# Attention beside a two-of-eight expert layer: tokens routed in parts of 12 and 20 tiles, the top two by maxima, another order of the set-up, the experts' tiles without a loop

## The chip, the cores and the metric

The kernel runs on one core of a Trainium2 chip, as one launch. The metric is the device time of an execution in microseconds (us). TensorE (PE, with its weight loads as PEld), VectorE (DVE), ScalarE (ACT), GpSimd (POOL) and SyncE (SP) each run a program of their own and meet at semaphores; a name with a q (PEldq, ACTq, SPq) is what an engine's sequencer does itself, such as loading a register or issuing a DMA.

## The reference

`x` is (4, 1024, 128), that is 4096 tokens or 32 tiles of 128. `xn` is its layer norm.

```
out  = x + attention(xn) + experts(xn)
attention: xn / max(|xn|, 1e-12) * sqrt(128) * gamma @ w_qkv, 16 heads of 64,
           causal softmax(q k^T / 8) v, @ w_out
experts:   logits = xn @ Wr^T + br                       # 8 experts
           top_v, top_i = top_k(logits, 2); w = softmax(top_v)
           o = sum over the two chosen e of w_e * (relu(xn @ W1[e]^T + b1[e]) @ W2[e]^T + b2[e])
           result = layer_norm(xn + o) * ffn_gamma + ffn_beta
```

Of two equal logits the expert with the lower number counts as the greater.

## The kernel before, in words

There are three stretches. In the **set-up** `x` is normed, the weights are turned by TensorE (a "unit" is four 128x128 transposes into one of four PSUM banks), the router chooses two experts a token, and GpSimd scatters each token's row twice into `sorted_x` in HBM, sorted by expert and padded to whole tiles of 128 rows. In the **expert stage** 78 tiles are run through the two layers of the expert that owns them. In the **attention** the 16 heads of 4 sequences follow, and the experts' rows are gathered back meanwhile. A barrier stands between the expert stage and the attention.

The routing is done in two parts of 16 tiles, `REGION = 2 * 16 + 7 = 39` sorted tiles each. For a part VectorE takes the statistics (L471, L474), norms (`layernorm`, L479 to L493), TensorE makes the logits, four tiles (a group) at a time, from a turned and copied `xn` (L658, L396, L667), `router` (L517 to L534) ranks the eight logits of a token against each other in 1024-wide operations (L521 to L526), TensorE counts the chosen (L673, L674), `places` (L540 to L563) makes every row's place of it, and GpSimd issues 32 indirect DMAs (L350). `experts_and_weights` (L570 to L579) gives `tile_expert`, the expert of each sorted tile, and the mixing weights.

What order the set-up has is the list `units`, which TensorE (`turn`), ScalarE (`evacuate`, plus `normed` and `exponentials`) and VectorE (`lower`) all walk: router and bias weights, `xn` of the first half, `w1` of all experts, `w2` of all, `n` (the normed rows for the attention) of the first half, then `xn` and `n` of the second. A bank of kind `w1` or `n` is read twice, by ScalarE (rounded) and then by VectorE (the rest, `w1T_lo` L504, `nT_lo` L508), and is free after that. TensorE waits for the last four banks before the expert stage.

In the expert stage every engine runs `step(j, k, i)` for tile j. On TensorE (L699 to L746) a step reads the expert's number from SBUF into a register (`expert_of`, L278), turns the rows of tile j+1 (L709), turns the hidden layer of tile j-1 (L727), multiplies tile j by W1 in three passes (L734 to L736) and tile j-2 by W2 (L743). `expert_steps` writes steps 0 to 2 out, runs steps 3 to 74 in a hardware loop of 12 rounds with 6 steps, and writes steps 75 to 80 out. In the last four steps of a round the register that was loaded two steps earlier serves W2 too; in the first two it is loaded anew. SyncE loads the sorted rows, three tiles a time, into two slots (L304).

```
inside = i is not None and k >= FIRST + 2
e_out = tile_experts[k - 2] if inside else expert_of(pe, j - 2)
```

## Time and profile before

| | us |
|---|---|
| three runs: median (lowest, highest) | 1506.33 (1504.99, 1508.04) |
| the profiled execution: its own time | 1506.04 |
| its span | 1504.3 |
| set-up, up to the first instruction of the expert stage | 0 to 94.88 |
| expert stage, up to the first matmul of the attention | 94.88 to 285.11 |
| attention | 285.11 to 1504.3 |
| TensorE, VectorE, ScalarE, GpSimd busy | 1389.7, 1119.1, 1057.4, 937.9 |

The times of a row are from one profiled execution; 1.7 us of its own time lie around its span. TensorE is busy nearly throughout the second and third stretches and less than half of the first. The granted clock is given as a share of full speed. Durations of matmuls overlap, so how often something happens is read from the starts.

### The profile page before, as it was taken

How to read it: one execution, taken by the hardware profiler on the slowest of the kernel's cores; microseconds unless marked ns; L12 is line 12 of the kernel's file. 1: busy time of each engine (PE TensorE's matmuls, PEld its weight loads, DVE VectorE, ACT ScalarE, POOL GpSimd, SP SyncE). 2: the span in 40 equal slices, each digit the busy share in tenths (PEclk: the TensorE clock that was granted, in tenths of full speed). 3: DMA queues.
4: the chain of work that ended last, by engine and by line, in shares of the span. 5: the costliest groups of instructions: out<-in, count | busy, mean ns of one | idle time of the engine just before them, and what ended most of it. 6: DMA issues, size and time to landing. Idle time of an engine off the chain costs nothing.

```text
span 1504.3 us, 27822 instructions
## 1 busy us (share of the span) xinstructions
PE 1389.7 (92%) x8618; PEld 1063.1 (71%) x8619; DVE 1119.1 (74%) x1933; ACT 1057.4 (70%) x2590; POOL 937.9 (62%) x921
## 2 busy tenths in 40 slices
PE   4559999789999999999999999999999999999996
PEld 3448888657777777777777777777777777777774
DVE  6565555457886789678868886888688869886984
ACT  2445655457777777777777777777777777777774
POOL 0663000139666966696669666966786678667775
PEclk9569999989999999999999999999999999999998
DMA  9122111212211221121122212221222122212112
GB/s 323 45 70 79 59 54 54 58 29 67 51 43 44 66 49 44 44 66 48 44 51 60 49 44 54 60 49 44 57 53 49 43 60 54 49 44 61 49 43 75
DMA packets 77188, 89.61 MB, mean 60 GB/s; under 512 B 17640, under 2 KB 54800, under 8 KB 77072
## 3 DMA queue, kind: packets, MB, share of 16 engines
q1 hardware_dynamic: 59152, 69.90, 18.4%
q10 hardware_dynamic: 13824, 9.86, 2.1%
q0 software_dynamic: 4096, 8.40, 1.9%
q8 instruction: 61, 1.00, 0.3%
q14 instruction: 55, 0.45, 0.1%
HBM read 37.25 MB, written 16.78 MB: 36 GB/s over the span
## 4 chain that ended last, share of the span: by engine, by line
PE 57%; DVE 11%; POOL 6%; issue 4%; ACT 2%; DMA 1%; SPq 0%; POOLq 0%; ACTq 0%
PE max_ps L1290 9%; PE head_ps L1332 7%; PE head_ps L1334 7%; PE head_ps L1336 7%; PE score_ps L1316 6%; PE score_ps L1315 6%; POOL p_lo L1056 4%; DVE row_max L1142 4%; PE misc_ps L1266 3%; PE misc_ps L1346 3%; POOL two_y L1049 2%; PE max_ps L1293 2%; PE misc_ps L1260 2%; PE score_ps L1318 2%; PE misc_ps L1262 2%
## 5 line engine op out<-in xcount | busy, mean ns | idle before, releaser
L1056 POOL TENSOR_TENSOR p_lo<-probs,p_hi 128x512 fp32r<-128x512 f32 (+3 forms) x768 | 806.1, 1068 | 320.9 <-ACT p_hi L1094 316.1
L1094 ACT ACTIVATE probs<-score_ps 128x512 f32<-128x512 f32 (+3 forms) x768 | 376.2, 490 | 210.7 <-PE score_ps L1318 115.6
L1142 DVE TENSOR_REDUCE row_max<-max_ps 128x1 f32<-128x128 f32 (+7 forms) x512 | 385.2, 754 | 170.4 <-PE max_ps L1293 165.6
L1094 ACT ACTIVATE p_hi<-score_ps 128x512 fp32r<-128x512 f32 (+3 forms) x768 | 375.5, 489 | 0.0
L1332 PE MATMUL head_ps<-p_hi,v_hi 128*65 128x512 f32 (+3 forms) x768 | 289.0, 376 | 2.6 <-POOL p_lo L1056 1.9
L1290 PE MATMUL max_ps<-k_a,q_a 128*128 128x384 f32 (+5 forms) x768 | 259.7, 393 | 26.1 <-DVE row_max L1142 20.9
L1315 PE MATMUL score_ps<-q_a,k_a 128*128 128x512 f32 (+3 forms) x768 | 266.5, 347 | 2.5 <-DMA q_b<-shift 2.4
L1316 PE MATMUL score_ps<-q_b,k_b 65*128 65x512 f32 (+3 forms) x768 | 267.4, 348 | 0.0
L1334 PE MATMUL head_ps<-p_hi,v_lo 128*64 128x512 f32 (+3 forms) x768 | 258.5, 337 | 0.0
L1336 PE MATMUL head_ps<-p_lo,v_hi 128*65 128x512 f32 (+3 forms) x768 | 258.5, 337 | 0.0
L1315 PEld LDWEIGHTS score_ps<-q_a,k_a 128*128 128x128 f32 x768 | 144.7, 188 | 45.1 <-issue 3.1
L1290 PEld LDWEIGHTS max_ps<-k_a,q_a 128*128 128x128 f32 x768 | 135.1, 198 | 43.0 <-DVE row_max L1142 32.7
L1316 PEld LDWEIGHTS score_ps<-q_b,k_b 65*128 65x128 f32 x768 | 145.5, 189 | 16.5
L1336 PEld LDWEIGHTS head_ps<-p_lo,v_hi 128*65 128x65 f32 x768 | 104.3, 136 | 42.3
L1332 PEld LDWEIGHTS head_ps<-p_hi,v_hi 128*65 128x65 f32 x768 | 108.7, 141 | 24.7 <-POOL p_lo L1056 8.0
L1334 PEld LDWEIGHTS head_ps<-p_hi,v_lo 128*64 128x64 f32 x768 | 105.1, 137 | 20.6
L1318 PE MATMUL score_ps<-later,ident 128*128 128x128 bf16 x512 | 118.7, 232 | 0.0
L1293 PE MATMUL max_ps<-ident,later 128*128 128x128 bf16 x512 | 118.5, 231 | 0.0
L1197 DVE TENSOR_TENSOR heads<-raw,scale 64x512 f32<-64x512 f32 x128 | 114.7, 896 | 4.1 <-DMA scale<-inv_rows 2.1
L1132 DVE TENSOR_TENSOR q_a<-misc_ps,q_a 64x512 fp32r<-64x512 f32 x128 | 88.2, 689 | 29.0 <-ACT q_a L1072 27.1
L432 ACT ACTIVATE w_raw<-bank,b1T 128x128 f32<-128x128 f32 x312 | 88.9, 368 | 21.7 <-PE bank L727 19.4
L350 POOL DMA_INDIRECT sorted_x<-xn,slots x64 | 62.5, 976 | 63.1 <-DVE slots L563 44.2
(166 smaller groups left out, 2178.0 us busy)
## 6 DMA issues: line engine op xcount, KB each, us to landing
k_a<-k_a SPq DMA_DIRECT2D x64, 256.0 KB, 3.9
q_b<-q_a SPq DMA_DIRECT2D x64, 256.0 KB, 4.7
scale<-inv_rows SPq DMA_DIRECT2D x128, 128.0 KB, 2.9
sorted_x<-zeros SPq DMA_DIRECT2D x13, 384.0 KB, 15.9
w_raw<-sorted_x SPq DMA_DIRECT2D x26, 192.0 KB, 2.5
sorted_y<-result ACTq DMA_DIRECT2D x78, 64.0 KB
acc<-in_L_attn_x_dram SPq DMA_DIRECT2D x4, 512.0 KB, 7.3
w_raw<-in_L_ffn_W_dram ACTq DMA_DIRECT2D x1, 2048.0 KB, 23.0
```

Of the source, the lines that this page charges most:

```text
L1056: pool.tensor_tensor(p_lo[:, slot, 0:w], probs[:, n_chunk(g, c) % PROBS, 0:w], p_hi[:, slot, 0:w].bitcast(F32), ALU.subtract).then_inc(p_s ...
L1094: ins = act.activation(p[:, n_chunk(g, c) % ring, 0:width], score_ps[n_chunk(g, c) % 2][:, 0:width], ACT.Exp, scale=SCALE)
L1142: dve.tensor_reduce(row_max[:, g % 2, t:t + 1], src, axes, ALU.max).then_inc(max_taken, 1)
L1197: dve.tensor_tensor(heads[s * HEAD:(s + 1) * HEAD, cols], raw[0:HEAD, s, half], scale[:, half], ALU.mult).then_inc(normalised, 1)
L1290: ins = pe.matmul(max_ps[:, b, 0:w], rows, k_a[i][s][:, k0:k0 + w], start=True, stop=not last)
L1293: ins = pe.matmul(max_ps[:, b, w - P:w], later[:], ident16[:], start=False, stop=True)
L1315: pe.matmul(dst, k_a[i][s][:, keys], q_a[i][s][:, qs], start=True, stop=False)
L1316: ins = pe.matmul(dst, k_b[i][s][:, keys], q_b[i][s][:, qs], start=False, stop=not DIAG[c])
L1318: ins = pe.matmul(dst[:, 0:P], ident16[:], later[:], start=False, stop=True)
L1332: pe.matmul(head_ps[0:HEAD + 1, cols], v_hi[i][:, j, s], p_hi[:, slot, 0:width], start=(j == 0), stop=False)
L1334: pe.matmul(head_ps[0:HEAD, cols], v_lo[i][:, j, s], p_hi[:, slot, 0:width], start=False, stop=False)
L1336: pe.matmul(head_ps[0:HEAD + 1, cols], v_hi[i][:, j, s], p_lo[:, slot, 0:width], start=False, stop=c in LAST).then_inc(pv_done, 1)
```

## The change

1. **Parts.** The first part has 12 tiles (31 sorted tiles), the second 20 (47). There are still 78 sorted tiles, and 64 indirect DMAs, now 24 and 40. Buffers that both parts used are doubled or kept per part. `sorted_x` is zeroed in 13 DMAs of the same size as before, each now one contiguous piece, and the first part waits only for the first 6.
2. **The best two.** `router` takes the greatest logit, marks those equal to it, picks the lowest numbered of them, lowers it by 3e38 and does the same again: 12 chained operations of 96 (or 160) elements and one for `chosen`, in place of five of 1024 and some smaller ones.
3. **Set-up order.** `units` is now: `xn` of three groups, `w1` and `w2` of experts 0 to 3, `xn` of five groups, `w2` 4 to 7, `n` of the first four groups, `w1` 4 to 7, `n` of the last four. `count(0)` stands ahead of the first `w1`, `count(1)` ahead of the first `n`. The ready signal of `xn` comes per group, and the five operations that give `nscale` stand behind the norming.
4. **The rest of `n`.** `nT_lo` is no longer made by VectorE from the bank, but by GpSimd from `nT`, behind all its scatters; the bank is free once ScalarE has read it.
5. **Tiles written out.** All 81 steps are written out, with no loop. On TensorE `inside` is now `i is not None`, which is never so: from step 2 on each step loads both registers. SyncE's loads are written out too.

```diff
-        REGIONS = 2
-        RT = ALL_TILES // REGIONS
-        REGION = 2 * RT + EXPERTS - 1
-        SORTED = REGIONS * REGION
+        CUT = [0, 12, ALL_TILES]
+        REGIONS = len(CUT) - 1
+        RT = [CUT[r + 1] - CUT[r] for r in range(REGIONS)]
+        MOST = max(RT)
+        REGION = [2 * n + EXPERTS - 1 for n in RT]
+        FIRST_TILE = [sum(REGION[:r]) for r in range(REGIONS + 1)]
+        SORTED = FIRST_TILE[REGIONS]
+        ZERO_TILES = 6
+        ZERO_CUT = [0, -(-REGION[0] // ZERO_TILES), SORTED // ZERO_TILES]
+        assert SORTED % ZERO_TILES == 0
...
-            units = [("wr", 0), ("b1", 0)]
-            for b in range(2):
-                for g in range(b * per_batch, (b + 1) * per_batch):
-                    units += [("xn", g)]
-            units += [("w1", e) for e in range(EXPERTS)] + [("w2", e) for e in range(EXPERTS)]
-            for b in range(2):
-                for g in range(b * per_batch, (b + 1) * per_batch):
-                    units += [("n", g)]
-            half_units = len(units)
-            for b in range(2, BATCH):
-                for g in range(b * per_batch, (b + 1) * per_batch):
-                    units += [("xn", g)]
-            for b in range(2, BATCH):
-                for g in range(b * per_batch, (b + 1) * per_batch):
-                    units += [("n", g)]
-            reads, n = {}, 0
-            for u, (kind, _) in enumerate(units):
-                if kind in ("w1", "n"):
-                    n += 1
-                    reads[u] = n
-
-            def tbank_counts(n):
-                return tbank[:, n * P:(n + 1) * P].rearrange("p (t e) -> p t e", e=EXPERTS)
+            GROUPS0 = RT[0] // GROUP
+            ALL_GROUPS = ALL_TILES // GROUP
+            units = ([("wr", 0), ("b1", 0)] + [("xn", g) for g in range(GROUPS0)]
+                     + [("w1", e) for e in range(4)] + [("w2", e) for e in range(4)]
+                     + [("xn", g) for g in range(GROUPS0, ALL_GROUPS)] + [("w2", e) for e in range(4, EXPERTS)]
+                     + [("n", g) for g in range(4)] + [("w1", e) for e in range(4, EXPERTS)]
+                     + [("n", g) for g in range(4, ALL_GROUPS)])
+            at_unit = {unit: u for u, unit in enumerate(units)}
+            w1_units = [u for u, (kind, _) in enumerate(units) if kind == "w1"]
...
             def expert_steps(eng, step):
 
-                for j in range(FIRST):
+                for j in range(SORTED + 3):
                     step(j, j, None)
-                with eng.Fori(0, LOOPS) as i:
-                    for k in range(UNROLL):
-                        step(i * UNROLL + (FIRST + k), FIRST + k, i)
-                for j in range(FIRST + LOOPS * UNROLL, SORTED + 3):
-                    step(j, j, None)
...
-                n = k // ring
-                return n if i is None else i * (UNROLL // ring) + n
+                return k // ring
...
-                    for i in range(13):
-                        sp.dma_start(flat[:, i * width:(i + 1) * width], zeros[:]).then_inc(zeroed, 16)
+                    for r in range(REGIONS):
+                        for i in range(ZERO_CUT[r], ZERO_CUT[r + 1]):
+                            part = sorted_x[i * ZERO_TILES * P:(i + 1) * ZERO_TILES * P, :]
+                            sp.dma_start(part.rearrange("(p a) d -> p (a d)", p=P), zeros[:]
+                                         ).then_inc(zeroed[r], 16)
...
+                    sp.wait_ge(turned, at_unit[("w2", 1)] + 1)
+                    for m, (a, b, r) in enumerate(LOADS):
+                        if a == FIRST_TILE[r]:
+                            sp.wait_ge(scattered[r], 16 * 2 * RT[r])
+                        if m >= 2:
+
+                            sp.wait_ge(rows_turned, LOADS[m - 1][0] + (LOAD + 1))
+                        sp.dma_start(rows[:, m % 2, 0:b - a], src[:, a:b]).then_inc(rows_loaded[m % 2], 16)
...
                     for r in range(REGIONS):
+                        for i in range(r + 1):
+                            pool.wait_ge(zeroed[i], 16 * (ZERO_CUT[i + 1] - ZERO_CUT[i]))
                         pool.wait_ge(slots_ready, r + 1)
-                        for t in range(r * RT, (r + 1) * RT):
+                        for t in range(CUT[r], CUT[r + 1]):
                             for n in range(2):
                                 pool.indirect_dma_start(
                                     sorted_x, bass.IndirectOffsetOnAxis(ap=slots[:, n, t:t + 1], axis=0),
                                     xn[:, t], None).then_inc(scattered[r], 16)
+                    for g in range(ALL_GROUPS):
+                        u = at_unit[("n", g)]
+                        cols = slice(g * BANK, (g + 1) * BANK)
+                        pool.wait_ge(bank_free[u % 4], freed(u))
+                        pool.tensor_tensor(nT_lo[:, cols], nT[:, cols], nT_hi[:, cols].bitcast(F32), ALU.subtract)
...
                     act.wait_ge(small_loaded, 16 * 4)
-                    for u in range(half_units):
-                        if u == units.index(("w1", 0)):
-                            for b in range(2):
-                                normed(b)
-                        if u == units.index(("w2", 0)):
+                    for u in range(len(units)):
+                        if units[u] == ("w1", 0):
+                            normed(0)
+                        if units[u] == ("w2", 0):
                             exponentials(0)
+                        if units[u] == ("w2", 4):
+                            normed(1)
+                        if units[u] == ("w1", 4):
+                            normed(2)
+                            normed(3)
+                            exponentials(1)
                         evacuate(u)
...
+                        then(dve.tensor_scalar(rstd[:, tiles], y[:, 0], 1.0, None, ALU.mult))
+                        for g in range(CUT[r] // GROUP, CUT[r + 1] // GROUP):
+                            for i in range(g * GROUP, (g + 1) * GROUP):
+                                ins = dve.tensor_scalar(xn[:, i], acc[:, i], mean[:, i:i + 1], rstd[:, i:i + 1],
                                                         ALU.subtract, ALU.mult)
                             ins.then_inc(xn_ready, 1)
-
-                    def lower(u):
...
+                        for place, values in ((0, bias), (1, rest)):
+                            top, mine = best[:, place, 0:n], pick[r][:, place]
+                            then(dve.tensor_reduce(top, values, AX_X, ALU.max))
+                            then(dve.tensor_tensor(ties, values, top.unsqueeze(2).broadcast_to(over), ALU.is_equal))
+                            then(dve.tensor_tensor(ties, ties, first_wins[:].unsqueeze(1).broadcast_to(over),
+                                                   ALU.mult))
+                            then(dve.tensor_reduce(won, ties, AX_X, ALU.max))
+                            then(dve.tensor_tensor(mine, ties, won.unsqueeze(2).broadcast_to(over), ALU.is_equal))
+                            if place == 0:
+                                then(dve.scalar_tensor_tensor(out=rest, in0=mine, scalar=LOWEST, in1=bias,
+                                                              op0=ALU.mult, op1=ALU.add))
+                        dve.tensor_tensor(chosen[:, 0:n], pick[r][:, 0], pick[r][:, 1],
+                                          ALU.add).then_inc(chosen_ready, 1)
+                        dve.tensor_tensor(gap[r][:], best[:, 1, 0:n], best[:, 0, 0:n],
+                                          ALU.subtract).then_inc(exp_asked, 1)
...
                     statistics(0)
                     layernorm(0)
                     statistics(1)
                     dve.wait_ge(small_loaded, 16 * 4)
-                    dve.wait_ge(set_up, 5)
+                    dve.wait_ge(set_up, 6)
                     router(0)
                     places(0)
+                    for e in range(4):
+                        lower(e)
                     layernorm(1)
-                    first = units.index(("w1", 4))
-                    for u in range(first):
-                        lower(u)
                     experts_and_weights(0)
-                    for u in range(first, half_units + 4):
-                        lower(u)
                     router(1)
                     places(1)
                     experts_and_weights(1)
                     dve.sem_inc(set_up, 1)
+                    for e in range(4, EXPERTS):
+                        lower(e)
                     dve.wait_ge(b2_loaded, 16)
-                    for u in range(half_units + 4, len(units)):
-                        lower(u)
                     w_lo(dve, 0)
...
+                    for u, (kind, n) in enumerate(units):
+                        if (kind, n) == ("w1", 0):
                             count(0)
-                        turn(u)
-                    for g in range(groups):
-                        turn(half_units + g)
-                        if g:
-                            logits(groups + g - 1)
-                    logits(2 * groups - 1)
-                    for u in range(half_units + groups, len(units)):
-                        if u == half_units + groups + 2:
+                        if (kind, n) == ("n", 0):
                             pe.wait_ge(slots_ready, 1)
                             count(1)
                         turn(u)
+                        if kind == "xn" and n not in (0, GROUPS0):
+                            logits(n - 1)
+                        if kind == "xn" and n in (GROUPS0 - 1, ALL_GROUPS - 1):
+                            logits(n)
...
-                            inside = i is not None and k >= FIRST + 2
+                            inside = i is not None
                             e_out = tile_experts[k - 2] if inside else expert_of(pe, j - 2)
```

The places that the prediction speaks of, as each engine's program has them. TensorE in the expert stage, one step in the loop of the kernel before (the fourth of a round), from its register load to the third pass of W1 (`lbank` and `tbank` hold turned rows, `bank` the hidden layer):

```order
L278 ISA
L278 TENSOR_LOAD tile_expert
L278 ISA x2
L709 MATMUL lbank<-ident,w_raw 128x128
L727 MATMUL bank<-ident,w_raw 128x128 x4
L731 REGISTER_ALU
L734 ISA
L734 MATMUL bank<-w1T_hi,rowsT_hi 128x512
L735 REGISTER_ALU
L735 MATMUL bank<-w1T_lo,rowsT_hi 128x512
L736 MATMUL bank<-w1T_hi,rowsT_lo 128x512
```

and one step of the changed kernel:

```order
L271 TENSOR_LOAD tile_expert
L271 ISA x2
L271 TENSOR_LOAD tile_expert
L271 ISA x2
L690 MATMUL lbank<-ident,w_raw 128x128
L708 MATMUL bank<-ident,w_raw 128x128 x4
L715 ISA
L715 MATMUL bank<-w1T_hi,rowsT_hi 128x512
L716 REGISTER_ALU
L716 MATMUL bank<-w1T_lo,rowsT_hi 128x512
L717 MATMUL bank<-w1T_hi,rowsT_lo 128x512
```

There is a second load of `tile_expert` with its two register operations, and the address operations ahead of the load and at L731 are gone.

ScalarE in the set-up before, from the scaled rows of the first half (`nrm`) to the first `n` unit (`nT`):

```order
L375 ACTIVATE nrm<-xn,nscale 128x128 x16
L385 ACTIVATE w1T_hi<-bank 128x512 x8
L405 ACTIVATE two<-gap 128x16
L398 ACTIVATE w2T<-bank 128x512 x8
L387 ACTIVATE nT<-bank,agamma 128x512
```

and in the changed kernel, the same place and then the end of the set-up:

```order
L367 ACTIVATE nrm<-xn,nscale 128x128 x8
L377 ACTIVATE w1T_hi<-bank 128x512 x4
L397 ACTIVATE second<-gap 128x12
L390 ACTIVATE w2T<-bank 128x512 x4
L388 ACTIVATE xnT<-bank 128x512 x5
L367 ACTIVATE nrm<-xn,nscale 128x128 x8
L390 ACTIVATE w2T<-bank 128x512 x4
```

```order
L367 ACTIVATE nrm<-xn,nscale 128x128 x16
L397 ACTIVATE second<-gap 128x20
L377 ACTIVATE w1T_hi<-bank 128x512 x4
L379 ACTIVATE nT<-bank,agamma 128x512
L380 ACTIVATE nT_hi<-bank,agamma 128x512
```

Scaled rows come in three pieces, and the last sixteen, the second exponential and four `w1` units stand between the first four `n` units and the last four.

VectorE in `router(1)` before, from the logits to the gap of the two best:

```order
L517 TENSOR_TENSOR logit<-lbank,br_all 128x128
L521 TENSOR_TENSOR more<-logit 128x1024
L522 TENSOR_TENSOR same<-logit 128x1024
L523 TENSOR_TENSOR same<-same,before 128x1024
L525 TENSOR_TENSOR more<-more,same 128x1024
L526 TENSOR_REDUCE rank<-more 128x128
L527 TENSOR_SCALAR chosen<-rank 128x128
L528 TENSOR_SCALAR pick<-rank 128x128
L529 TENSOR_SCALAR pick<-rank 128x128
L531 TENSOR_TENSOR prod<-pick,logit 128x256
L533 TENSOR_REDUCE two<-prod 128x32
L534 TENSOR_TENSOR gap<-two 128x16
```

and now, without the two last operations:

```order
L504 TENSOR_TENSOR logit<-lbank,br_all 128x160
L508 TENSOR_REDUCE best<-logit 128x20
L509 TENSOR_TENSOR tied<-logit,best 128x160
L510 TENSOR_TENSOR tied<-tied,first_wins 128x160
L512 TENSOR_REDUCE winner<-tied 128x20
L513 TENSOR_TENSOR pick<-tied,winner 128x160
L515 SCALAR_TENSOR_TENSOR logit<-pick,logit 128x160
L508 TENSOR_REDUCE best<-logit 128x20
L509 TENSOR_TENSOR tied<-logit,best 128x160
L510 TENSOR_TENSOR tied<-tied,first_wins 128x160
L512 TENSOR_REDUCE winner<-tied 128x20
L513 TENSOR_TENSOR pick<-tied,winner 128x160
```

The chain has more operations, and none is wider than 160 elements.

## Rows read from the trace of the kernel before

**Rows 1.** Set-up, expert stage, attention: busy us (instructions) of each engine, TensorE's clock, DMA

```profile
0.00:94.88 94.88, 40.64 (x202) 37.71 (x204) 61.94 (x220) 34.61 (x81) 39.30 (x53) 0.72 0.46 158
94.88:285.11 190.23, 176.34 (x1248) 157.61 (x1249) 98.04 (x234) 110.43 (x390) 25.96 (x29) 0.98 0.20 61
285.11:1504.30 1219.19, 1172.71 (x7168) 867.83 (x7168) 959.11 (x1479) 912.33 (x2119) 872.69 (x841) 0.99 0.21 52
```

**Rows 2.** Timeline of VectorE in the set-up: start, length, instruction, [idle before]

```profile
28.83 0.29 DVE L517 TENSOR_TENSOR logit<-lbank,br_all 128x128 f32<-128x128 f32 x1 [4.12 <-PE lbank L667]
...
35.33 0.23 DVE L527 TENSOR_SCALAR chosen<-rank 128x128 f32<-128x128 f32 x1
...
36.86 0.28 DVE L540 COPY totals<-tbank 128x128 f32<-128x128 f32 x1
...
38.25 0.22 DVE L551 TENSOR_TENSOR small<-before,tiles_of 128x64 f32<-128x64 f32 x1
...
41.14 0.18 DVE L563 CAST slots<-two_f 128x32 uint32<-128x32 f32 x1
...
45.30 4.18 DVE L493 TENSOR_SCALAR xn<-acc,mean,rstd 128x128 f32<-128x128 f32 x16
...
90.80 2.73 DVE L508 SCALAR_TENSOR_TENSOR nT_lo<-bank,agamma,nT_hi 128x512 fp32r<-128x512 f32 x4 [0.21 <-DVE weights L579]
```

**Rows 3.** Timeline of ScalarE in the set-up

```profile
26.01 4.77 ACT L375 ACTIVATE nrm<-xn,nscale 128x128 f32<-128x128 f32 x16
...
30.69 2.15 ACT L385 ACTIVATE w1T_hi<-bank 128x512 fp32r<-128x512 f32 x4
...
62.27 0.73 ACT L387 ACTIVATE nT<-bank,agamma 128x512 f32<-128x512 f32 x1
...
63.41 0.74 ACT L387 ACTIVATE nT<-bank,agamma 128x512 f32<-128x512 f32 x1
...
70.43 0.60 ACT L396 ACTIVATE xnT<-bank 128x512 f32<-128x512 f32 x1 [2.42 <-PE bank L658]
...
72.88 0.60 ACT L396 ACTIVATE xnT<-bank 128x512 f32<-128x512 f32 x1 [1.86 <-PE bank L658]
```

**Rows 4.** Timeline of GpSimd and of SyncE's queue in the set-up

```profile
42.26 1.20 POOL L350 DMA_INDIRECT sorted_x<-xn,slots  x1 [38.78 <-DVE slots L563]
...
82.57 0.96 POOL L350 DMA_INDIRECT sorted_x<-xn,slots  x1 [0.30 <-issue]
...
85.23 1.10 SPq L304 DMA_DIRECT2D w_raw<-sorted_x  x2
```

**Rows 5.** Timeline of TensorE in the expert stage, the turning of one tile's rows

```profile
94.88 0.47 PE L709 MATMUL tbank<-ident,w_raw 128*128 128x128 f32 x1 [9.01 <-issue]
...
104.19 0.32 PE L709 MATMUL tbank<-ident,w_raw 128*128 128x128 f32 x1 [0.30 <-issue]
...
161.22 0.32 PE L709 MATMUL tbank<-ident,w_raw 128*128 128x128 f32 x1 [0.61 <-issue]
...
163.79 0.32 PE L709 MATMUL lbank<-ident,w_raw 128*128 128x128 f32 x1 [0.20 <-issue]
...
166.00 0.27 PE L709 MATMUL tbank<-ident,w_raw 128*128 128x128 f32 x1
...
168.14 0.27 PE L709 MATMUL lbank<-ident,w_raw 128*128 128x128 f32 x1
...
273.93 0.32 PE L709 MATMUL tbank<-ident,w_raw 128*128 128x128 f32 x1 [0.20 <-issue]
...
276.13 0.33 PE L709 MATMUL lbank<-ident,w_raw 128*128 128x128 f32 x1
```

**Rows 6.** Line 278 on TensorE's sequencer: count, ns min/median/max, first to last start

```profile
L278 PEldq TENSOR_LOAD <-tile_expert x108: 296/302/552, 93.9 to 281.1; - x108
...
L278 PEldq TENSOR_LOAD <-tile_expert x2: 296/302/309, 274.8 to 275.5; - x2
...
L278 PEldq TENSOR_LOAD <-tile_expert x2: 296/298/300, 277.0 to 277.7; - x2
```

More of the change, by code:

```diff
@@ L21 @@
 MASKED = -1e30
+LOWEST = -3e38
 def attention_and_experts(nc, x, attn_gamma, w_qkv, w_out, w_router, b_router,
@@ new lines, in attention_and_experts @@
+            chosen = sb(ph1, "chosen", [P, MOST, EXPERTS])
+            pick = [sb(ph1, f"pick{r}", [P, 2, RT[r], EXPERTS]) for r in range(REGIONS)]
+            prod = [sb(ph1, f"prod{r}", [P, 2, RT[r], EXPERTS]) for r in range(REGIONS)]
+            two_f = [sb(ph1, f"two_f{r}", [P, 2, RT[r]]) for r in range(REGIONS)]
+            gap = [sb(ph1, f"gap{r}", [P, RT[r]]) for r in range(REGIONS)]
+            second = [sb(ph1, f"second{r}", [P, RT[r]]) for r in range(REGIONS)]
+            upto = [sb(ph1, f"upto{r}", [P, EXPERTS, RT[r]]) for r in range(REGIONS)]
@@ L202, in attention_and_experts @@
+            totals = [sb(ph1, f"totals{r}", [P, EXPERTS, RT[r]]) for r in range(REGIONS)]
             tiles_int = sb(ph1, "tiles_int", [P, EXPERTS], I32)
```

277 lines of the change are left out of this document (115 added, 162 removed).

## The prediction

> **What bounds the kernel now.** I read the split by stretches first [rows 1]. The change touches only the set-up (94.88 us) and the expert stage (190.23 us); the attention's code is the same, so its 1219.19 us stay. TensorE is busy for 176 of the expert stage's 190 us, but for only 41 of the set-up's 95 us: the set-up is a chain of hand-overs. Next I read that chain on VectorE and ScalarE [rows 2, 3], the scatters that hang on it [rows 4], and the rhythm of the tiles on TensorE [rows 5] with what its sequencer does in a step [rows 6]. In a hand-over, see the idle time in brackets: VectorE stood 4.12 us before its first router operation because the logits were not there. In the expert stage, see that the start of L709 moves by 2.14 us from one step to the next where a step has one register load (166.00 to 168.14), and that the gap before 161.22 is "issue": TensorE waits for its own sequencer.
>
> **The set-up, first part.** Router(0) began at 28.83, after four groups of logits. The groups follow one another at 2.45 us, read from ScalarE's copies of the turned rows (70.43, 72.88) [rows 3]. Three groups instead of four: 28.83 - 2.45 = 26.4. VectorE is there in time, since it idled 4.12 us before and has the same statistics and fewer normings in front. The router before took 35.33 + 0.23 - 28.83 = 6.7 us to `chosen` [rows 2]. The new chain has 12 dependent operations of 96 elements and one more. Such widths are not in the trace; 64 elements took 0.22 and 128 took 0.29, so I take 0.255, and allow 0.04 between dependent ones. Bounds are 0.22 and 0.29, half a microsecond over the chain. 12 x 0.295 + 0.26 = 3.8, so `chosen` is there at 30.2. From `chosen` to the end of `places` it was 41.32 - 35.56 = 5.8; three quarters of the width takes about 0.5 off: 35.5. So the first slots come 5.8 us earlier, of which the router gives 2.9.
>
> GpSimd began 0.94 us after the slots and issued every (82.57 - 42.26) / 31 = 1.30 us [rows 4]. 24 instead of 32: from 36.4, the last at 66.3. SyncE loaded 2.66 us behind the last issue: 69.0. That is no limit if the set-up ends later than some 72, and it does. Zeroing was no wait before either (the scatter followed VectorE), and now only six pieces are ahead.
>
> **Second part.** Behind `places(0)` VectorE has four `lower` of 512 elements, and four operations of that width took 2.73 (L508) [rows 2]: 38.2. From there to the first `xn` it was 45.30 - 41.32 = 4.0; five operations move behind (1.1), so 2.9: 41.1. Norming takes 4.18 / 16 = 0.26 a tile: the first group is ready at 42.2 and the fifth at 46.3. Five groups of logits at 2.45, and some 0.9 for the first to be turned: router(1) starts at 55.3, against 76.1 before, because it no longer stands behind all of `w1`, `w2` and half of `n`. At 160 elements I take 0.325 by the same slope (the 128-wide 0.29 below, twice that above, 3.5 us on the chain): 12 x 0.365 + 0.33 = 4.7, `chosen` at 60.0. `count(1)` takes 36.86 - 35.56 = 1.3: 61.3, and an estimated 1 us goes to turning the first `n` unit (a group's 2.45 holds turning and logits): 62.3.
>
> From here ScalarE is the last to finish. It has four `n` units at 63.41 - 62.27 = 1.14 each (4.6), 16 scaled tiles (4.77), an exponential (0.2), four `w1` units (2.15) and four more `n` units (4.6) [rows 3]: 16.3 us, ending at 78.6. VectorE's four `lower` and TensorE's turning lie beside these. `nT_lo` is off this path: it goes to GpSimd behind the scatters, where nothing runs for the rest of the expert stage (25.96 us busy of 190) [rows 1], so it costs nothing up to some 130 us for eight. Before, the last `nT_lo` ended at 90.80 + 2.73 = 93.53 and the first L709 came at 94.88, 1.35 later [rows 2, 5]. So the expert stage starts at **80.0**, 14.9 us earlier. Bounds: 77 if the groups of logits run faster, 86 if ScalarE is held up between its pieces as it was before.
>
> Later scatters are no limit: 40 issues from 67.3 end at 119.3, and tile 31 is turned at about 80.0 + 9.3 + 27 x 2.2 = 148.7, so 29 us are spare. If `slots(1)`, which I expect at 60.0 + 6.2 = 66.2, came 29 us later, this would turn into a wait.
>
> **The expert stage.** The loop goes, and a second register load comes into four of six steps; the work of the array is the same 78 tiles. Steps 3 to 74 took 273.93 - 104.19 = 169.7 us, 2.36 each [rows 5]. The first two steps of a round, those with two loads and the loop's branch, cost more than the other four. What is a written-out step with two loads worth? The kernel before has such steps, behind its loop. From 273.93 to 276.13 it is 2.20, and the pairs of loads that belong to them start 274.8 and 277.0, again 2.2 [rows 6]: the sequencer's own period, just above the 2.14 of a one-load step. So a second load of 0.30 and its register operations nearly fit into the time that the sequencer has to spare. 72 x 2.20 = 158.4, a gain of **11.3**. The bounds are 2.14 (the array) and 2.57 (163.79 - 161.22, a loop step with two loads and with computed addresses, which the written-out steps lack). I take the tail's value since its instructions are, one by one, those of the new steps; 2.57 has more of them.
>
> The Trainium skill says in "DMA: Bandwidth & Descriptors", "Latency and other measured facts", that a `tensor_load` has a floor of about 600 ns and that the compiler unrolls to spread it. The loads here take 302 ns at the median [rows 6], so this trace does not agree. By the page's figure two loads would add 0.6 us to each step, an estimate of 43 us more, and the kernel would be slower.
>
> SyncE's written-out loads cost nothing: a load of three tiles is asked for when the slot's tiles are turned, three steps ahead. The single-tile load at the parts' seam (tile 30) still leaves two steps, 4.4 us.
>
> **The sum.** Start 80.0, steps 0 to 2 as before (104.19 - 94.88 = 9.3), 158.4, and 285.11 - 273.93 = 11.2 to the attention: it begins at 258.9 instead of 285.11, 26.2 us earlier. The profiled execution took 1506.04, 0.3 under the median of the three: 1506.04 - 26.2 = **1479.8**.
>
> **Rivals.**
> - *Two loads nearly for nothing fails.* Place: TensorE's sequencer, in each of 72 steps. The loop's own two-load step costs 2.57; with that in all, the stage is 9.3 + 185.0 + 11.2 = 205.5 and the attention starts at 285.5: 1506.4, no change. If a load also cost what the dearest of the 108 did, 0.55 instead of 0.30 [rows 6], a step would be 2.20 + 0.50 = 2.70, the stage 214.9, the start 294.9: **1515.8**, slower. It decides from 2.57 a step on. For it: the sequencer has no slack left. Against it: the tail's step, with the very same instructions, took 2.20. The page of the Trainium skill named above speaks for this rival.
> - *Set-up gain halved.* ScalarE's or VectorE's chain in the second part is held up, and the expert stage starts at 87: **1487**. For it: in the kernel before ScalarE's pieces stood apart by 2.42 and 1.86 us [rows 3]; my chain has ten hand-overs. Against it: from 62 on ScalarE's inputs are all there ahead.
> - *The second load is hidden altogether*, 2.14 a step: **1475.5**. Against it the tail's 2.20.
> - *The change does not do what it says*, that is the start of the expert stage stays bound by the end of the second part's routing, as if parts did not matter. This holds even in my forecast (78.6 against 72 for the first rows), so 12 and 20 tiles give less than the new order.
>
> **How the numbers follow.** Forecast 77%, set-up halved 12%, fully hidden load 5%, step at 2.57 or more 6%, of which two thirds slower. A measurement of this kernel tells about 0.2%, 3 us, from no change. Own range of the forecast: 77 to 83 for the start and 2.16 to 2.25 a step, 1474 to 1486. To hold eight in ten with the second case, 1472 to 1491. Faster 94%, same 2%, slower 4%.
>
> **What would show it.** Logits of the first router at about 26, slots at 35 and 66, the last copy of `n` by ScalarE at 78 to 79, first turned row at 80; L709 at steps of 2.20 with pairs of loads 2.2 apart; first matmul of the attention at 259 and 1219 us from there to the end. The prediction is wrong if the steps' starts move by over 2.3, if GpSimd's last scatter of the first part ends behind 78, or if the attention's length changes.

## The result, and the profile after

| | before | after |
|---|---|---|
| median of the runs, us (lowest, highest) | 1506.27 (1504.99, 1508.04), 4 runs | 1486.22 (1484.01, 1489.48), 4 runs |
| ratio, 95% interval | | 0.9868 [0.9853, 0.9884] |
| profiled execution: own time, span | 1506.04, 1504.3 | 1485.95, 1484.2 |

The kernel became 20 us faster, 1.3%. The forecast was 1479.8, 26.2 us less than the profiled execution of before; the time lies in the wide range given (1472 to 1491), 6.4 us above the forecast and at the upper edge of the forecast's own range (1474 to 1486). The 20.1 us between the two spans are split by the stretches, which answer to [rows 1]:

```profile
0.00:80.66 80.66, 42.99 (x203) 39.28 (x203) 49.48 (x215) 35.05 (x80) 37.08 (x55) 0.83 0.53 184
80.66:263.81 183.15, 179.47 (x1249) 160.95 (x1249) 99.35 (x234) 110.89 (x390) 38.38 (x39) 0.97 0.22 66
263.81:1484.20 1220.39, 1174.38 (x7168) 868.86 (x7168) 955.99 (x1479) 912.73 (x2119) 872.28 (x841) 0.99 0.21 52
```

The set-up is 14.2 us shorter, the expert stage 7.1, the attention 1.2 longer. VectorE has 12.5 us less to do in the set-up, and GpSimd 12.4 more in the expert stage, 9.9 of them for the rests of `n`. That VectorE's chain runs earlier shows in its timeline, in the same columns as [rows 2]:

```profile
25.96 0.26 DVE L504 TENSOR_TENSOR logit<-lbank,br_all 128x96 f32<-128x96 f32 x1 [4.41 <-PE lbank L657]
...
29.44 0.26 DVE L517 TENSOR_TENSOR chosen<-pick 128x96 f32<-128x96 f32 x1
...
34.88 0.18 DVE L551 CAST slots<-two_f 128x24 uint32<-128x24 f32 x1
...
55.05 0.33 DVE L504 TENSOR_TENSOR logit<-lbank,br_all 128x160 f32<-128x160 f32 x1 [5.93 <-PE lbank L657]
...
66.22 0.28 DVE L551 CAST slots<-two_f 128x40 uint32<-128x40 f32 x1
```

The first `chosen` is there at 29.7 (35.56 before), the first slots at 35.06 (41.32). VectorE idles 5.93 us ahead of the second router: TensorE's and ScalarE's groups of logits pace that piece. ScalarE's queue, against [rows 3]:

```profile
62.10 0.69 ACT L379 ACTIVATE nT<-bank,agamma 128x512 f32<-128x512 f32 x1 [3.02 <-PE bank L647]
...
66.68 4.79 ACT L367 ACTIVATE nrm<-xn,nscale 128x128 f32<-128x128 f32 x16
71.35 0.23 ACT L397 ACTIVATE second<-gap 128x20 f32<-128x20 f32 x1
71.46 2.06 ACT L377 ACTIVATE w1T_hi<-bank 128x512 fp32r<-128x512 f32 x4
74.62 0.69 ACT L379 ACTIVATE nT<-bank,agamma 128x512 f32<-128x512 f32 x1 [1.11 <-PE bank L647]
...
78.63 0.73 ACT L380 ACTIVATE nT_hi<-bank,agamma 128x512 fp32r<-128x512 f32 x1
```

From 62.1 on the row at 74.62 has the only wait of some length, 1.11 us ahead of the last four `n` units. It ends at 79.36, and the expert stage starts 1.3 us behind it. That wait has a chain of its own:

```profile
71.68 0.36 DVE L566 TENSOR_SCALAR gap<-second 128x20 f32<-128x20 f32 x1 [4.02 <-ACT second L397]
72.72 2.48 DVE L494 TENSOR_TENSOR w1T_lo<-bank,w1T_hi 128x512 fp32r<-128x512 f32 x4
73.47 3.56 PE L647 MATMUL bank<-ident,nrm 128*128 128x128 f32 x16 [5.92 <-DVE w1T_lo L494]
```

VectorE waits 4.02 us for ScalarE's `second` to make the mixing weights, and only then makes `w1T_lo`. The first of these frees the bank for which TensorE has stood 5.92 us. TensorE then turns the first of the last four `n` units at a granted clock of 0.50 (its mean from 70 to 76 us), and ScalarE gets it at 74.62. The scatters and the first load, against [rows 4]:

```profile
35.93 1.19 POOL L336 DMA_INDIRECT sorted_x<-xn,slots  x1 [32.05 <-DVE slots L551]
...
65.55 0.97 POOL L336 DMA_INDIRECT sorted_x<-xn,slots  x1 [0.30 <-issue]
...
67.86 0.91 SPq L301 DMA_DIRECT2D w_raw<-sorted_x  x2
...
117.94 9.93 POOL L343 TENSOR_TENSOR nT_lo<-nT,nT_hi 128x512 fp32r<-128x512 f32 x8
```

The rows are asked for at 67.86, 12.8 us ahead of their use, so the scatters are off the path. `nT_lo` follows the last scatter and is done at 127.9. Last TensorE, against [rows 5], and its register loads, against [rows 6]:

```profile
80.66 0.47 PE L690 MATMUL tbank<-ident,w_raw 128*128 128x128 f32 x1 [3.63 <-issue]
...
90.94 0.27 PE L690 MATMUL tbank<-ident,w_raw 128*128 128x128 f32 x1
...
200.96 0.31 PE L690 MATMUL lbank<-ident,w_raw 128*128 128x128 f32 x1
203.19 0.32 PE L690 MATMUL tbank<-ident,w_raw 128*128 128x128 f32 x1
205.51 0.33 PE L690 MATMUL lbank<-ident,w_raw 128*128 128x128 f32 x1
...
252.52 0.33 PE L690 MATMUL tbank<-ident,w_raw 128*128 128x128 f32 x1
...
L271 PEldq TENSOR_LOAD <-tile_expert x156: 295/300/498, 79.8 to 259.9; - x156
```

Here 90.94 is step 3 and 252.52 step 75: 72 steps in 161.58 us, 2.244 each, against 2.36 before. The first step takes 2.13 and the others 2.18 to 2.40; the two shown take 2.23 and 2.32.

### The profile page after: what moved, and what is told of

It reads as the page before. It is cut to its first block, busy times and chain, and to the rows that moved or that the text cites. A ratio compares the mean times of both kernels' runs of the same rounds, so it can differ in the third digit from the quotient of the medians.

```text
span 1484.2 us, 27052 instructions
## 1 busy us (share of the span) xinstructions
PE 1396.8 (94%) x8618; PEld 1069.1 (72%) x8618; DVE 1104.8 (74%) x1928; ACT 1058.7 (71%) x2589; POOL 947.7 (64%) x933
## 4 chain that ended last, share of the span: by engine, by line
PE 58%; DVE 11%; POOL 6%; issue 4%; ACT 2%; DMA 1%; SPq 0%; POOLq 0%
PE max_ps L1271 9%; PE head_ps L1313 7%; PE head_ps L1315 7%; PE head_ps L1317 7%; PE score_ps L1297 7%; PE score_ps L1296 6%; DVE row_max L1123 4%; POOL p_lo L1037 4%; PE misc_ps L1247 3%; PE misc_ps L1327 3%; POOL two_y L1030 2%; PE max_ps L1274 2%; PE misc_ps L1241 2%; PE score_ps L1299 2%; PE misc_ps L1243 2%
## 5 line engine op out<-in xcount | busy, mean ns | idle before, releaser
L1271 PE MATMUL max_ps<-k_a,q_a 128*128 128x384 f32 (+5 forms) x768 | 259.8, 393 | 26.2 <-DVE row_max L1123 20.8
L1178 DVE TENSOR_TENSOR heads<-raw,scale 64x512 f32<-64x512 f32 x128 | 118.0, 922 | 4.0 <-DMA scale<-inv_rows 2.0
L1274 PEld LDWEIGHTS max_ps<-ident,later 128*128 128x128 bf16 x512 | 49.6, 97 | 67.1 <-issue 50.1
```

The costliest lines, as they stand in the source:

```text
L1178: dve.tensor_tensor(heads[s * HEAD:(s + 1) * HEAD, cols], raw[0:HEAD, s, half], scale[:, half], ALU.mult).then_inc(normalised, 1)
L1271: ins = pe.matmul(max_ps[:, b, 0:w], rows, k_a[i][s][:, k0:k0 + w], start=True, stop=not last)
L1274: ins = pe.matmul(max_ps[:, b, w - P:w], later[:], ident16[:], start=False, stop=True)
```

## The experiments

Two questions were open: what sets the 2.244 us of a step, and what of the set-up's gain belongs to which part of the change. Below, "step" is the mean of steps 3 to 74, read as above, and "start" the first turned row of the expert stage. Ratios are to the kernel before, run beside each. The set-up's code is the same in the changed kernel, e1, e5 and e9, and their starts lie between 79.07 and 80.91: a difference in the start under some 2 us between two rows is not told from chance. Runs e1 to e4, e5 to e8, and e9 with e10 shared a chip each.

| | median us | ratio [interval] | start | steps 0 to 2 | step | attention's start, length |
|---|---|---|---|---|---|---|
| before | 1506.27 | | 94.88 | 9.31 | 2.358 | 285.11, 1219.2 |
| after | 1486.22 | 0.9868 [0.9853, 0.9884] | 80.66 | 10.28 | 2.244 | 263.81, 1220.4 |
| e1 one load | 1477.55 | 0.9799 [0.9782, 0.9815] | 80.91 | 9.11 | 2.140 | 255.10, 1221.4 |
| e2 even parts | 1487.89 | 0.9875 [0.9858, 0.9891] | 85.50 | 9.45 | 2.248 | 268.05, 1218.7 |
| e3 before, written out | 1499.28 | 0.9948 [0.9931, 0.9964] | 94.70 | 9.09 | 2.253 | 277.35, 1219.4 |
| e4 before, two loads | 1520.39 | 1.0086 [1.0065, 1.0107] | 95.75 | 9.52 | 2.531 | 298.66, 1218.3 |
| e5 three loads | 1530.63 | 1.0160 [1.0143, 1.0177] | 80.10 | 10.54 | 2.887 | 309.75, 1218.3 |
| e6 ranked | 1489.20 | 0.9888 [0.9871, 0.9904] | 85.31 | 9.54 | 2.248 | 267.96, 1218.9 |
| e7 rest on VectorE | 1485.96 | 0.9861 [0.9845, 0.9877] | 80.43 | 10.48 | 2.247 | 263.92, 1220.9 |
| e8 one load, filled | 1475.66 | 0.9805 [0.9784, 0.9826] | 80.04 | 7.19 | 2.140 | 252.35, 1220.0 |
| e9 one load again | 1475.30 | 0.9796 [0.9782, 0.9810] | 79.07 | 10.39 | 2.140 | 254.54, 1219.0 |
| e10 filled again | 1476.11 | 0.9796 [0.9783, 0.9810] | 80.38 | 7.16 | 2.141 | 252.67, 1221.4 |

### One register load a step (e1)

```diff
-                            inside = i is not None
+                            inside = k >= 4
```

> The changed kernel, but from step 4 on TensorE takes the expert's number for W2 from the register loaded two steps earlier, so a step has one register load. Theory A (the written-out step is paced by TensorE's sequencer, which two loads fill): L690 moves by 2.15 us a step instead of 2.24, the 72 steps take 154.8 instead of 161.6, and the time is 6.5 to 7 us below the changed kernel's 1486.2, about 1479.5. Theory B (the 2.24 comes from fetching the written-out instructions): the step stays at 2.2 or above and the time within 3 us of 1486.2.

Every step became 2.14, without a single exception:

```profile
201.29 0.27 PE L690 MATMUL tbank<-ident,w_raw 128*128 128x128 f32 x1
203.43 0.27 PE L690 MATMUL lbank<-ident,w_raw 128*128 128x128 f32 x1
205.57 0.27 PE L690 MATMUL tbank<-ident,w_raw 128*128 128x128 f32 x1
```

The time is 2 us below theory A's 1479.5; steps 0 to 2, 1.2 us shorter than in the changed kernel, are the larger part of that, and are within chance (e9). So the second load is what makes a step of the changed kernel 0.10 us longer and uneven. That the code is written out does not: e1's is too. It is the fastest form here, with and without the unused matmuls that e8 and e10 add to it: some 9 us under the changed kernel and 30 under the one before.

### Three register loads (e5)

```diff
                             e_out = tile_experts[k - 2] if inside else expert_of(pe, j - 2)
+                            if 3 <= j < 75:
+                                expert_of(pe, j - 2)
```

> The changed kernel with a third, unused register load on TensorE in each of the steps 3 to 74. If the sequencer's own period sets the step, each load beyond the first adds what a load takes there: the load is 0.30 us at the median, with its register operations 0.3 to 0.47, so a step goes from 2.244 to 2.54 to 2.71 and the kernel to 1507 to 1520 us. If the 0.10 us between a one-load step (2.14) and a two-load step (2.244) came from something other than a full sequencer, the third load adds about 0.10 again: 2.35 a step, 1494 us.

```profile
200.82 0.32 PE L690 MATMUL tbank<-ident,w_raw 128*128 128x128 f32 x1 [0.57 <-issue]
203.73 0.32 PE L690 MATMUL lbank<-ident,w_raw 128*128 128x128 f32 x1 [0.56 <-issue]
206.54 0.32 PE L690 MATMUL tbank<-ident,w_raw 128*128 128x128 f32 x1 [0.46 <-issue]
```

Now the turned row waits half a microsecond for "issue", that is for its own sequencer, which confirms the kind of limit for three loads. The rows of the two-load kernel name no such wait; that its sequencer is full too follows from e1, where one load less makes all steps alike. The size is more than either theory gave: 2.887 - 2.244 = 0.643 us for one load more, though the record of the load itself is 0.30 and its register operations 0.15 and 0.02:

```profile
L271 PEldq TENSOR_LOAD <-tile_expert x2: 302/332/363, 202.4 to 203.0; - x2
L271 PEldq FUSED_REGOPS  x1: 151/151/151, 202.7 to 202.7; - x1
L271 PEldq SEQ_ASSERT  x1: 18/18/18, 203.0 to 203.0; - x1
```

These are TensorE's sequencer operations between 202.41 and 203.10: count, ns (least, median, most), first and last start. From one load to the next it is 202.4 to 203.0, 0.6 us, while the three records add up to 0.47: the rest lies between them. If the second load costs the sequencer as much as the third, which no run tried apart, the sequencer needs 2.244 - 0.643 = 1.60 us for a one-load step, 0.54 less than the array's 2.14. The second load then uses up these 0.54 and shows the last 0.10; the third shows in full. The Trainium skill gives in "DMA: Bandwidth & Descriptors", "Latency and other measured facts", a floor of about 600 ns for a `tensor_load`. The record of one load, 300 to 302 ns at the median, does not agree with it; the 0.643 us that one more costs here, register operations included, is near it.

### The kernel before, written out, and with two loads in its loop (e3, e4)

```diff
-                for j in range(FIRST):
-                    step(j, j, None)
-                with eng.Fori(0, LOOPS) as i:
-                    for k in range(UNROLL):
-                        step(i * UNROLL + (FIRST + k), FIRST + k, i)
-                for j in range(FIRST + LOOPS * UNROLL, SORTED + 3):
+                for j in range(SORTED + 3):
                     step(j, j, None)
```

> The kernel before with nothing changed but the experts' steps, all written out with two loads. Both theories leave the set-up at 94.9. If the written-out steps are worth what the changed kernel shows (2.36 to 2.24 us, 72 times), the stage loses 8 us and the time is about 1498. If the 2.20 of the tail holds when only this is changed, 11 us: 1495. If the parts' seam or the scatters beside it cost the rest, it shows here as a lower step than 2.24.

```diff
-                            inside = i is not None and k >= FIRST + 2
+                            inside = False
```

> The kernel before, with its loop, but both registers loaded anew in every step. Theory A (in a loop the computed addresses make the second load dear): the four cheap steps of a round go from 2.15 to 2.57 us, 12 x 4 x 0.42 = 20 us more, about 1526. The rival (a second load costs 0.1 us in the loop too): 5 us more, 1511.

Writing out alone gives 8.3 us by the medians (1507.61 before in these runs) and moves no part of the set-up: the expert stage's gain stands by itself, and its step is that of the changed kernel. Two loads in all steps of the loop cost 12.8 us, between the two theories. A stretch of it:

```profile
193.98 0.33 PE L709 MATMUL lbank<-ident,w_raw 128*128 128x128 f32 x1
196.88 0.33 PE L709 MATMUL tbank<-ident,w_raw 128*128 128x128 f32 x1 [0.55 <-issue]
199.45 0.32 PE L709 MATMUL lbank<-ident,w_raw 128*128 128x128 f32 x1 [0.21 <-issue]
201.97 0.33 PE L709 MATMUL tbank<-ident,w_raw 128*128 128x128 f32 x1 [0.15 <-issue]
204.36 0.32 PE L709 MATMUL lbank<-ident,w_raw 128*128 128x128 f32 x1
206.73 0.32 PE L709 MATMUL tbank<-ident,w_raw 128*128 128x128 f32 x1
```

The steps here are 2.90 (the one at the loop's branch), 2.57, 2.52, 2.39 and 2.37; their mean over the loop is 2.531, against 2.253 written out. Two loads fill the sequencer's time already in a written-out step (e1, e5), so nothing is left in which the branch and the computed addresses could hide: the loop costs 0.28 us a step. How these 0.28 divide between the two was not tried.

### Even parts (e2)

```diff
-        CUT = [0, 12, ALL_TILES]
+        CUT = [0, 16, ALL_TILES]
```

> The changed kernel with parts of 16 and 16 tiles. Theory A (the smaller first part is what lets the new order count): the first router waits for a fourth group of logits (28.4 instead of 26.0), slots at 38, 32 scatters of 1.27 us end at 80, the rows arrive at about 84.5 and the expert stage starts at about 85, 4 to 5 us later: 1490.5. Theory B (the parts don't matter, the second part's set-up is the limit either way): start at 80.7 and 1486.2.

```profile
82.86 6.14 SPq L301 DMA_DIRECT2D w_raw<-sorted_x  x3
...
85.50 0.48 PE L690 MATMUL tbank<-ident,w_raw 128*128 128x128 f32 x1 [8.71 <-DMA w_raw<-sorted_x]
```

The start is the one that theory A expected, and the wait has the expected name: TensorE idles 8.71 us for the sorted rows, though ScalarE is through at 79.27. The attention begins 4.2 us later than in the changed kernel. By the ratios the two are not told apart (0.9875 against 0.9868); in its profiled execution the attention, whose code is the same, was 1.7 us shorter. So the 4.8 us stand in the trace and are not told apart in the total, which at 1487.89 is 2.6 under theory A's.

### The router of before (e6)

Both parts use the ranking again, in the buffers and the order of the changed kernel:

```diff
-                        for place, values in ((0, bias), (1, rest)):
...
+                        then(dve.tensor_tensor(sa, other, mine, ALU.is_equal))
+                        then(dve.tensor_tensor(sa, sa, before[:].unsqueeze(1).broadcast_to(shape4), ALU.mult))
+                        then(dve.tensor_tensor(mo, mo, sa, ALU.add))
+                        then(dve.tensor_reduce(ra, mo, AX_X, ALU.add))
```

> The changed kernel with the router of the kernel before (all pairs ranked against each other) in both parts. Theory: the router is on the path twice over, but only the second part's counts for the start, since ScalarE's last pieces hang on chosen(1). With 20 tiles the ranking takes 6.7 x 20/16 = about 8.2 us where the maxima took 4.7: slots of the first part 2 us later (37), chosen of the second part 3.5 us later (63.2), expert stage from 84.2 instead of 80.7, 1489.7 us. Rival: the first router's delay adds to the second's, start at 86 and 1491.5 us. Rival: ScalarE's pieces have enough other work, start at 81 and 1486 us.

```profile
56.23 0.33 DVE L508 TENSOR_TENSOR logit<-lbank,br_all 128x160 f32<-128x160 f32 x1 [6.09 <-PE lbank L663]
56.59 1.49 DVE L514 TENSOR_TENSOR nT<-logit 128x1280 f32<-128x1280 f32 x1
...
64.09 0.24 DVE L519 TENSOR_SCALAR chosen<-rank 128x160 f32<-128x160 f32 x1
```

The second router takes 64.33 - 56.23 = 8.1 us and begins 1.2 later than with the maxima. ScalarE's first `n` unit moves from 62.10 to 66.78 and the start from 80.66 to 85.31, both by 4.7: the chain from `chosen(1)` over ScalarE to the start is what the forecast took it for. Of these 4.7, 3.5 are the second router's own (8.1 us against 4.6) and 1.2 come from the first. That the delay adds up over both routers, the first rival, is so, and its start (86) is the nearest of the three; by the time the theory (1489.7) is nearer. The median, 1489.20, is 3.0 us above the changed kernel's, with 0.9888 against 0.9868, where the intervals overlap.

### The rests of `n` on VectorE again (e7)

```diff
-                        pool.wait_ge(bank_free[u % 4], freed(u))
-                        pool.tensor_tensor(nT_lo[:, cols], nT[:, cols], nT_hi[:, cols].bitcast(F32), ALU.subtract)
...
+                        dve.wait_ge(act_read, w1_units.index(u) + 1)
+                        dve.scalar_tensor_tensor(out=nT_lo[:, cols], in0=bank[u % 4][:], scalar=agamma[:, 0:1],
+                                                 in1=nT_hi[:, cols].bitcast(F32), op0=ALU.mult, op1=ALU.subtract)
```

> The changed kernel with nT_lo made by VectorE from the bank again instead of by GpSimd behind its scatters. Theory: at the end of the set-up the bank is free one VectorE operation later (0.68 us), so the expert stage starts at 81.4 and the kernel takes 1487 us. If VectorE's queue (places of the second part, four w1T_lo) holds the banks up as it did in the kernel before, ScalarE's pieces come apart: start at 84, 1489.5 us. Rival: moving it was worth nothing, 80.7 and 1486.2 us.

The start is 80.43 and the ratio 0.9861, which is what the rival said and not the theory. Why, the end of the set-up shows:

```profile
74.95 0.75 DVE L490 SCALAR_TENSOR_TENSOR nT_lo<-bank,agamma,nT_hi 128x512 fp32r<-128x512 f32 x1 [0.26 <-ACT nT_hi L375]
76.10 0.75 DVE L490 SCALAR_TENSOR_TENSOR nT_lo<-bank,agamma,nT_hi 128x512 fp32r<-128x512 f32 x1 [0.40 <-ACT nT_hi L375]
...
77.65 0.73 ACT L375 ACTIVATE nT_hi<-bank,agamma 128x512 fp32r<-128x512 f32 x1
78.42 0.75 DVE L490 SCALAR_TENSOR_TENSOR nT_lo<-bank,agamma,nT_hi 128x512 fp32r<-128x512 f32 x1 [0.40 <-ACT nT_hi L375]
```

VectorE waits for ScalarE each time and ends at 79.17, 0.79 us behind ScalarE's 78.38, and the start comes 1.26 behind VectorE. So the theory's operation does stand on the path. It does not show in the start because ScalarE ended 0.98 earlier than in the changed kernel: its first `n` unit came 0.32 earlier (61.78), and its wait ahead of the last four was 0.47 us instead of 1.11. TensorE had idled 2.93 us there instead of 5.92, and its granted clock from 72 to 74 us was 0.88 instead of 0.50; that this shortened the wait was not tried apart. In the new order the move to GpSimd is worth nothing that the start or the ratio shows, and a loss or gain of 0.8 us is below what they can tell.

### TensorE kept busy ahead of the expert stage (e8, e9, e10)

Two unused matmuls stand behind each unit from the second `n` on, and two behind each wait for one of the last four banks, in the kernel of e1:

```diff
+                    def fill(times_):
+                        for _ in range(times_):
+                            pe.matmul(lbank[:].rearrange("p t e -> p (t e)")[:, 0:P], ones[:], earlier[:],
+                                      start=True, stop=True)
...
+                        if u > at_unit[("n", 0)]:
+                            fill(2)
...
                         pe.wait_ge(bank_free[u % 4], freed(u))
+                        fill(2)
```

> The changed kernel with one register load a step, and with two unused 128-wide matmuls on TensorE behind each unit from the second n unit on and behind each wait for one of the last four banks. In the changed kernel the granted clock is at its lower level (1.2 GHz) from 82 to 90 us, and the first three steps take 10.3 us where the kernel before took 9.3; with one load they take 9.1. If it is TensorE's idling ahead of the expert stage that lets the clock fall, the filled kernel keeps the higher level, and steps 0 to 2 take about 7.5: 1476 us against 1477.5 with one load alone. Rival: the fillers hold up the units, the start moves from 80.9 to 82 and nothing is won: 1478.5 us.

The changed kernel's windows around the start of the expert stage, columns as in [rows 1] (the last but two is the granted clock):

```profile
78.00:82.00 4.00, 0.78 (x3) 0.39 (x3) 0.93 (x3) 2.16 (x6) 3.08 (x4) 0.77 0.14 49
82.00:86.00 4.00, 3.43 (x10) 2.53 (x11) 0.89 (x2) 0.69 (x3) 3.09 (x4) 0.50 0.34 98
86.00:90.00 4.00, 3.43 (x12) 2.43 (x12) 1.04 (x3) 2.16 (x8) 3.02 (x4) 0.50 0.16 53
90.00:94.00 4.00, 4.00 (x31) 3.82 (x31) 2.20 (x5) 1.78 (x7) 2.90 (x3) 0.95 0.21 66
```

And those of the filled kernel (e10):

```profile
78.00:82.00 4.00, 3.02 (x22) 2.49 (x21) 0.91 (x3) 2.05 (x6) 3.04 (x4) 1.00 0.14 49
82.00:86.00 4.00, 2.92 (x16) 1.80 (x16) 1.87 (x4) 1.67 (x6) 3.08 (x4) 1.00 0.33 106
86.00:90.00 4.00, 4.00 (x31) 3.61 (x30) 1.97 (x4) 2.56 (x9) 3.09 (x4) 1.00 0.22 73
```

In the changed kernel TensorE was nearly idle ahead of 82 us and then works at 0.50, the 1.2 GHz level, up to 90. Filled, it is at 1.00, 2.4 GHz, in all three windows, and the first three steps take 7.2 us in both runs, instead of 9.11 and 10.39 in the same kernel without fillers (e1, e9). That the idling ahead of the stage makes its first steps slow is shown. Whether it pays is not: to tell that, both kernels ran again side by side.

> The same kernel as e1 (one register load a step), on the same chip as the filled one: 1477.5 us again.

> The same kernel as e8 (one register load a step and unused matmuls ahead of the expert stage), against the one without them on the same chip. In the two profiles its attention began 2.75 us earlier, so it should be 2 to 3 us under the other: 1475 us. If the earlier clock is given back behind the expert stage, both take the same.

The attention began 1.9 us earlier with the fillers (252.67 against 254.54), but it was 2.4 us longer in that profiled execution, and the ratios are the same, 0.9796 both. The medians, 1475.30 without and 1476.11 with the fillers, lie the other way round from what was expected. Over the four executions of these two kernels the attention took 1221.4 and 1219.0 without fillers and 1220.0 and 1221.4 with them, so that it gives the gain back is not shown either. A gain of 2 us is at the edge of what these runs can tell, and this one is not seen in them.

## Why the prediction was right, and where it was off

Its direction, its range and the mechanism of both gains held: the set-up became shorter along the chain that it followed, and the written-out steps carry a second load for 0.10 us. Two of its steps were wrong in part, the price of a load and the end of ScalarE's chain. Of the 6.1 us by which it was too good (a gain of 26.2, measured 20.1 on the spans):

- **The step: 3.2 us.** The term was 72 x 2.20, measured 72 x 2.244. This is the mis-sized term. It was read from one step of the tail, 273.93 to 276.13 [rows 5], and the written-out steps run from 2.18 to 2.40 but for the first; one step near the low end was taken for the mean. Behind it stands the price of a load: the prediction took the record, 0.30 us and its register operations, and e5 shows 0.643. Its own rows had the larger price: in a pair, the second load starts 0.7 us behind the first (274.8 and 275.5, 277.0 and 277.7 [rows 6]). That the pairs are 2.2 apart, which it took for the sequencer's own period, says nothing of that, since they must be as far apart as the steps whatever sets these. The forecast escaped with 0.044 a step, in part by luck, because most of the load's price has cover (e1, e5). Its upper bound of 2.57 holds for a loop's step with two loads (2.531 in e4), and the loop's part of that, 0.28, is what a written-out step does not have.
- **The attention: 1.2 us.** Nothing was changed there. Over the profiled executions of the table its length goes from 1218.3 to 1221.4 and for one and the same kernel from 1219.0 (e9) to 1221.4 (e1), so nothing shows that this part has a cause in the change. The prediction had named a change of this length as a sign of being wrong; 1.2 us is within what one kernel shows.
- **Steps 0 to 2: 1.0 us.** Taken as before at 9.3, measured 10.28. One and the same kernel takes 9.11 (e1) and 10.39 (e9), so this is within chance. The lower clock is no part of the difference, since the kernel before starts the stage at 0.50 too; without it they take 7.2 (e8, e10).
- **The start: 0.7 us.** 80.0 forecast, 80.66 measured. By pieces: router(0) 26.4 and 25.96, `chosen` 30.2 and 29.7, slots(0) 35.5 and 35.06, router(1) 55.3 and 55.05, first `n` unit 62.3 and 62.1, last piece of ScalarE 78.6 and 79.36. The widths that no row of before had were sized well: 0.26 and 0.33 us for 96 and 160 elements against 0.255 and 0.325. Up to 62.1 the chain was thus 0.2 to 0.5 early, and behind it 1.0 longer than forecast. What was missing is the 1.11 us that ScalarE idled for a turned bank at 74.62. The prediction held that from 62 on ScalarE's inputs are all there ahead and that VectorE's `lower` and TensorE's turning lie beside; in fact ScalarE's `second`, VectorE's weights and `w1T_lo` and TensorE's turning form a loop back to ScalarE there.
- **The tail: 0.1 us**, 11.2 forecast and 11.29 measured.

What the set-up's 14.2 us are made of, each undone alone: the router 4.7 (e6), the uneven parts 4.8 (e2), `nT_lo` on GpSimd nothing that shows (e7), each from one profiled execution, where one kernel's start varies by 1.8. These do not have to add up, and the other edits (the order of the units, the ready signal per group, the zeroing in two lots) were not tried one by one, so if they do add up, the rest of some 4.7 us is theirs together. The sentence that "12 and 20 tiles give less than the new order" rests on the rows coming ahead of the set-up's end, and leaves out that with even parts they would not: then the start moves to 85.5, since the last of the first part's 32 scatters is issued at 80.5, behind ScalarE's 79.27. The uneven cut shows in the start as much as the router does. Whether the new order gives more than that was not run.

The rivals: the step at 2.57 or more did not come, nor the set-up at 87, nor the second load altogether hidden; the steps' starts and the start of the expert stage in the table rule them out. The Trainium skill's floor of some 600 ns for a `tensor_load` ("DMA: Bandwidth & Descriptors", "Latency and other measured facts") spoke for the dear load: by it the prediction estimated 0.6 us more a step. Its 43 us count all 72 steps, though only 48 of them, four in six, gained a load; on these the same estimate gives 29. The second load added 0.10 (e1), and the third, with no cover left, 0.643 (e5). So the price was about right and the cover, which that estimate left out, kept it from showing.

## What to carry to other kernels

Where a step is paced by the array, a register load on the sequencer is free while the sequencer has time to spare in a step, and then it shows whole (2.140, 2.244 and 2.887 us for one, two and three loads): count it by what one more costs (0.64 us here), not by its record (0.30), and keep the register where an unrolled program allows it. When a chain is shortened, price its edits by undoing each in the new kernel: here one that was a limit before (the rests of `n` on VectorE) showed no cost any more, and one that looked minor (the cut of the parts) did. A single instance of a step is no mean; take the first and the last of many.

## What the runs showed of the hardware

- One register load more on TensorE's sequencer costs 0.643 us in a step that the sequencer bounds (e5), and 0.10 on top of a one-load step (e1), which by these numbers has an estimated 0.54 us to spare; the record of the load says 0.30.
- The same kernel's attention stretch differed by 2.4 us (1219.0 and 1221.4) between two executions, the start of its expert stage by 1.8 (79.07 and 80.91) and its first three steps by 1.3 (9.11 and 10.39; all e9 and e1), as much as the smaller effects here. Compare such effects at the place where they arise, and in more than one execution.
- TensorE's granted clock was 0.50 from 82 to 90 us, in the expert stage's first steps behind an idle stretch, and 1.00 from 78 on when it was given unused matmuls in that stretch (e10). The first three steps took 7.2 us instead of 9.1 to 10.4.
- GpSimd issued its indirect DMAs every 1.27 to 1.28 us, and took 1.24 us for a difference of 512 elements in SBUF (9.93 for 8) where VectorE's operation for the same rest, from a PSUM bank, took 0.75 (e7).
